# Graph network on one core: norms of the third and fourth layer from column statistics, degree scales moved ahead of the products

## What is computed

```python
def _layernorm(x):                       # over the 64 columns
    return (x - mean(x)) / sqrt(var(x) + 1e-5)

# block 1, in the kernel's edge phase: one 64x64 weight for each of 16 edge types
# block 2, three times (kernel layers 0, 1 and 2):
agg = segment_sum(h[src], dst) / max(cnt, 1)
h = agg @ Wl[i] + h @ Wr[i] + b[i]       # relu after the first two only
# block 3 (kernel layer 3):
feat_n = feat * rsqrt(out_deg)
h_src = feat_n[src]
copy_sum  = segment_sum(h_src, dst)
inner_sum = segment_sum(h_src * feat_n[dst], dst)
rst = (copy_sum @ weight1 + inner_sum @ weight2) * rsqrt(in_deg)
# block 4: two attention layers
```

## Time and profile before

| what | before |
|---|---|
| median of 3 runs | 6825.58 us (6820.51 to 6826.78) |
| the profiled execution, its time | 6816.61 us |
| the profiled execution, its span | 6814.9 us |
| busy: DVE, POOL, PE, ACT | 69%, 64%, 55%, 29% |
| third layer, first gather to first gather of the fourth | 2902.78 to 3559.78 us |
| fourth layer, first gather to the gather after it | 3559.78 to 4270.23 us |
| first layer, first to last gather | 1725.5 to 2254.1 us |
| third layer, first to last gather | 2902.8 to 3489.8 us |
| fourth layer, first to last gather | 3559.8 to 4190.3 us |

### The profile page before, as it was taken

One profiled execution on the slowest core, in us unless ns is written; L12 is line 12 of the kernel. 1 busy time (PEld: TensorE's weight loads), 2 busy tenths in 40 slices (PEclk: granted clock), 3 DMA queues, 4 the chain that ended last, 5 costly groups with the idle time before them and its releaser, 6 DMA issues. The chain is left out here.

```text
span 6814.9 us, 77215 instructions
## 1 busy us (share of the span) xinstructions
PE 3721.7 (55%) x19512; PEld 2540.9 (37%) x19512; DVE 4669.2 (69%) x16700; ACT 1956.3 (29%) x4823; POOL 4358.8 (64%) x4027
## 2 busy tenths in 40 slices
PE   3776888884588587723322333466378746661000
PEld 1443555552355455523322332355245423330000
DVE  7998999995455355446655676555699957776543
ACT  0000677775111111111111111122122258881000
POOL 5777777777677577577747784777200066664777
PEclk9999999997555556555555555777655678885555
DMA  1112344332233233234433433223133355552221
GB/s 37 49 48 75 125 157 145 111 104 82 71 105 89 66 105 89 82 108 129 129 111 92 122 107 109 87 88 94 68 139 129 137 114 130 131 138 75 83 88 71
DMA packets 413603, 684.89 MB, mean 100 GB/s; under 512 B 283685, under 2 KB 290444, under 8 KB 407978
## 3 DMA queue, kind: packets, MB, share of 16 engines
q1 hardware_dynamic: 282410, 542.14, 22.4%
q0 software_dynamic: 130944, 140.05, 10.4%
HBM read 310.94 MB, written 373.78 MB: 100 GB/s over the span
## 5 line engine op out<-in xcount | busy, mean ns | idle before, releaser
L697 POOL DMA_INDIRECT G<-states,srcq x1568 | 1761.7, 1124 | 528.0 <-issue 515.3
L1113 DVE TENSOR_TENSOR_SCAN R<-same,R,G 128x28 f32<-128x28 f32 x5376 | 990.0, 263 | 737.7 <-DMA G<-states,srcq 733.5
L1731 PE MATMUL PS<-ident,HH 128*128 128x128 f32 x2357 | 546.5, 392 | 1580.9 <-DVE HH L1275 684.9
L1731 PEld LDWEIGHTS PS<-ident,HH 128*128 128x128 f32 x2357 | 430.5, 215 | 1627.9 <-DVE HH L1275 700.5
L1998 ACT COPY AT<-PS 128x512 f32<-128x512 f32 (+1 forms) x494 | 287.7, 583 | 1983.5 <-PE PS L1731 1325.9
L697 POOL DMA_INDIRECT G<-states_xl,dsti x392 | 455.0, 1161 | 227.4 <-issue 122.0
L811 POOL DMA_INDIRECT out_nodes<-O,dstq x392 | 432.8, 1104 | 195.5 <-issue 123.3
L1746 PEld LDWEIGHTS PS<-WD,AT 128*128 128x128 f32 x2358 | 483.7, 305 | 123.6 <-issue 122.1
L1746 PE MATMUL PS<-WD,AT 128*128 128x64 f32 x2358 | 520.6, 398 | 1.1 <-ACT O L2009 0.7
L697 POOL DMA_INDIRECT G<-states,srci x392 | 421.7, 1076 | 124.3 <-issue 124.3
L697 POOL DMA_INDIRECT EE<-node_info,srcq x392 | 412.7, 1053 | 132.3 <-issue 132.3
(11 more groups left out here) (386 smaller groups left out, 9029.2 us busy)
## 6 DMA issues: line engine op xcount, KB each, us to landing
states<-O SPq DMA_DIRECT2D x70, 896.0 KB, 3.7
HH<-states SPq DMA_DIRECT2D x56, 896.0 KB
total<-R SPq DMA_DIRECT2D x56, 896.0 KB, 3.7
XB<-resid SPq DMA_DIRECT2D x42, 896.0 KB, 5.8
states<-HH SPq DMA_DIRECT2D x28, 896.0 KB
G<-states,srcq POOLq DMA_INDIRECT x1568
resid<-XB SPq DMA_DIRECT2D x28, 896.0 KB, 6.8
xl_of_src<-O SPq DMA_DIRECT2D x14, 1792.0 KB, 6.9
```

The costliest lines, as they stand in the source:

```text
L697: return pool.indirect_dma_start(to, None, table_, bass.IndirectOffsetOnAxis(ap=idx, axis=0), bounds_check=bound, oob_is_err=False).then_i ...
L1113: last = dve.tensor_tensor_scan(out=out_[:, order, f], data0=flags[:, order], data1=in_[:, order, f], initial=initial[:, f:f + 1], op0=ALU ...
L1731: last = pe.transpose(PS[:, 4 + k, q * P:(q + 1) * P], HH[:, b, (g * G4 + q) * D2:(g * G4 + q + 1) * D2], ident[:])
```

## The change

It touches the third and the fourth layer, the weights' loads and ACT's program.

- `new_states` takes the place of `new_state` for the 28-column chunks. DVE adds `O` to `XB`, takes mean and variance of each column by 28 `bn_stats` of 64 values, and works on tiles of 28 values after that. The norm itself is 28 `activation`s on ACT (`Relu(scale * x + bias)`, one for each column), spread in sevens over the group steps 4 to 7 of the next chunk's products (`normed_before`). The patch row keeps the old `norm`.
- The third layer's bias goes through PE, as in the first two: `lastb` and its addition are gone, `BS` has three rows.
- In the fourth layer ACT multiplies the loaded right halves by `rs_dst`, 28 `activation`s for each chunk, four to a group step of the chunk before (`scaled`). DVE waits for these (`s_rscaled`) and no longer for the load. `rs_in` is multiplied into the sums where the left halves are written, so that the copy and the scaling of `O` are gone.
- ACT's loops of these layers are written out, chunk by chunk.

```diff
@@ operands
                 if k < 3:
                     return tt(left, r, per_row(inv_in, i, INV_FT, n), ALU.mult)
-                step(tt(right, right, per_row(rs_dst, i, RSDST_FT, n), ALU.mult))
-                step(tt(right, right, r, ALU.mult))
-                return cast(left, r)
-
-            def new_state(k, layer, i, b, n):
-
-                o, xb = O[:, b, 0:n * D], XB[:, b, 0:n * D]
-                if k == 3:
-                    step(tt(cut(o), cut(o), per_row(rs_in, i, RSIN_FT, n), ALU.mult))
-                else:
-                    step(tt(cut(o), cut(o), lastb[:].unsqueeze(1).broadcast_to([P, n, D]), ALU.add))
+                step(tt(left, r, per_row(rs_in, i, RSIN_FT, n), ALU.mult))
+                if n == 1:
+                    step(tt(right, right, over(col(RSDST_FT), D), ALU.mult))
+                return tt(right, right, left, ALU.mult)
+
+            def new_states(k, layer, i, b):
+
+                total_, spread_, dev, inv, shift, diff = RLN
+                at = RNORMS + (k - 2) * CHUNKS + i
+                step(tt(XB[:, b, :], XB[:, b, :], O[:, b, 0:CD], ALU.add))
+                for j in range(C):
+                    last = dve.bn_stats(RSTATS[:, j, :], XB[:, b, j * D:(j + 1) * D])
+                step(last)
...
+                tt(spread_, spread_, diff, ALU.add).then_inc(s_vars, 1)
+                dve.wait_ge(s_devs, at + 1)
+                dve.wait_ge(s_done, before[layer, "done"] + i)
+                step(dve.reciprocal(inv, dev))
+                dve.scalar_tensor_tensor(out=shift, in0=total_, scalar=-0.5, in1=inv, op0=ALU.mult, op1=ALU.mult).then_inc(s_scales, 1)
@@ state
-                    dve.wait_ge(s_ld[b], before[layer, "ld"] + 16 * (it + 1))
+                    if k == 3:
+                        dve.wait_ge(s_rscaled, i + 1)
+                    else:
+                        dve.wait_ge(s_ld[b], before[layer, "ld"] + 16 * (it + 1))
@@ PE
-                how = (WD[:, k, :], BS[:, k, :], D) if k < 2 else (WD[:, k, :] if k == 2 else W12[:], None, D)
+                how = (WD[:, k, :], BS[:, k, :], D) if k < 3 else (W12[:], None, D)
@@ ACT
+                def scaled(i, groups):
+                    b = i % 2
+                    for g in groups:
+                        if g == 0:
+                            act.wait_ge(s_ld[b], before[layer, "ld"] + 16 * (i // 2 + 1))
+                        for j in range(g * G4, (g + 1) * G4):
+                            right = HH[:, b, j * D2 + D:(j + 1) * D2]
+                            last = act.activation(right, right, ACT.Copy, scale=rs_dst[:, i * C + j:i * C + j + 1])
+                        if g == GROUPS - 1:
+                            last.then_inc(s_rscaled, 1)
+
+                def normed_before(i, b, g):
...
+                    if g == 2:
+                        act.wait_ge(s_vars, at)
+                        act.activation(dev, spread_, ACT.Sqrt, bias=epsc[:], scale=1.0 / D).then_inc(s_devs, 1)
+                    if 4 <= g < 8:
+                        if g == 4:
+                            act.wait_ge(s_scales, at)
+                        for j in range((g - 4) * (C // 4), (g - 3) * (C // 4)):
+                            last = act.activation(O[:, b, j * D:(j + 1) * D], XB[:, b, j * D:(j + 1) * D], ACT.Relu,
+                                                  bias=shift[:, j:j + 1], scale=inv[:, j:j + 1])
+                        if g == 7:
+                            last.then_inc(s_done, 1)
```

More of the change, by code:

```diff
@@ L61 @@
 EPS = 1.0e-5
-WEIGHT_LOADS = 34
+WEIGHT_LOADS = 33
 HSLOT = 3 * (HI + 1) + 2 * 256
@@ L164, in build_program @@
         WG2 = sb("WG2", [P, D2])
[L165 removed]
+        BS = sb("BS", [1, 3, D])
         BG2 = sb("BG2", [1, D2])
@@ L306, in node_units @@
             return [(stage, w) for stage, w in made if 0 <= w < NGROUPS]
+        RSTATS = flat[2][:, 0:6 * C].rearrange("p (c k) -> p c k", k=6)
+        RLN = [flat[2][:, (6 + k) * C:(7 + k) * C] for k in range(6)]
+        RNORMS = len(NORMS)
         NROUNDS = NGROUPS + 4
@@ L332, in build_program @@
             plan(layer, ld=TURNS * 16, res=normed * TURNS * 16, st=(1 + normed) * TURNS * 16, tot=TURNS * 16, gath=TURNS * 16 * C,
-                 scan=CHUNKS, ready=CHUNKS + 1, group=GROUPS * CHUNKS + 1, done=(CHUNKS + 1) * normed, ln=normed * (CHUNKS + 1), carry=1,
+                 scan=CHUNKS, ready=CHUNKS + 1, group=GROUPS * CHUNKS + 1, done=(CHUNKS + 1) * normed, ln=normed, carry=1,
                  patch=(2 + normed) * 16, patched=(1 + normed) * 16)
@@ L1275, in operands, with new_first @@
                     return tt(left, r, per_row(inv_in, i, INV_FT, n), ALU.mult)
-                step(tt(right, right, per_row(rs_dst, i, RSDST_FT, n), ALU.mult))
-                step(tt(right, right, r, ALU.mult))
-                return cast(left, r)
-            def new_state(k, layer, i, b, n):
-                o, xb = O[:, b, 0:n * D], XB[:, b, 0:n * D]
-                if k == 3:
-                    step(tt(cut(o), cut(o), per_row(rs_in, i, RSIN_FT, n), ALU.mult))
-                else:
-                    step(tt(cut(o), cut(o), lastb[:].unsqueeze(1).broadcast_to([P, n, D]), ALU.add))
+                step(tt(left, r, per_row(rs_in, i, RSIN_FT, n), ALU.mult))
[9 more added lines that the diff above has]
+                step(last)
+                dve.wait_ge(s_scales, at)
+                tt(total_, RSTATS[:, :, 1], RSTATS[:, :, 4], ALU.add)
+                tt(spread_, RSTATS[:, :, 2], RSTATS[:, :, 5], ALU.add)
+                step(tt(diff, RSTATS[:, :, 1], RSTATS[:, :, 4], ALU.subtract))
+                step(dve.scalar_tensor_tensor(out=diff, in0=diff, scalar=D / 4.0, in1=diff, op0=ALU.mult, op1=ALU.mult))
+                tt(spread_, spread_, diff, ALU.add).then_inc(s_vars, 1)
[3 more added lines that the diff above has]
+                dve.scalar_tensor_tensor(out=shift, in0=total_, scalar=-0.5, in1=inv, op0=ALU.mult, op1=ALU.mult).then_inc(s_scales, 1)
+            def new_first(layer):
+                o, xb = O[:, 0, 0:D], XB[:, 0, 0:D]
                 step(tt(xb, xb, o, ALU.add))
-                norm(xb, o, n, before[layer, "ln"] + 1 + i).then_inc(s_done, 1)
+                norm(xb, o, 1, before[layer, "ln"] + 1).then_inc(s_done, 1)
             for b in range(2):
@@ L1313, in finish @@
                     dve.wait_ge(s_out, before[layer, "group"] + AHEAD + GROUPS * (i + 1))
-                    new_state(k, layer, i, b, C)
+                    new_states(k, layer, i, b)
                 def source_hots(i):
@@ L1365, in _ @@
                     dve.wait_ge(s_out, before[layer, "group"] + AHEAD + GROUPS * CHUNKS + 1)
-                    new_state(k, layer, CHUNKS, 0, 1)
+                    new_first(layer)
                 barrier()
@@ L2028, in free @@
                                                                 (i - b) // 2 * 16 * (1 + normed)))
-                def norm_before(i, g):
-                    if g == 2:
-                        square(C, before[layer, "ln"] + i)
-                    if g == 4:
-                        root(C, before[layer, "ln"] + i)
+                def scaled(i, groups):
[9 more added lines that the diff above has]
+                def normed_before(i, b, g):
+                    at = RNORMS + (k - 2) * CHUNKS + i
+                    total_, spread_, dev, inv, shift, diff = RLN
+                    if g == 2:
+                        act.wait_ge(s_vars, at)
[8 more added lines that the diff above has]
+                            last.then_inc(s_done, 1)
                 put = out_rows(ACT.Relu if k < 2 else ACT.Identity, free)
@@ L2039, in _, with beside @@
                     act.activation(rs_dst[:], SRC_P, ACT.Sqrt).then_inc(s_deg, 1)
-                if normed:
-                    products(layer, copy, put)(0, None, 0)
-                    body = products(layer, copy, put, norm_before)
-                    with act.Fori(0, TURNS - 1) as it:
-                        body(2 * it + 1, it, 1)
-                        body(2 * it + 2, it, 0)
-                    body(CHUNKS - 1, None, 1)
-                    norm(C, before[layer, "ln"] + CHUNKS)
+                if k == 3:
+                    scaled(0, range(GROUPS))
+                    for i in range(CHUNKS):
+                        def beside(i, g):
+                            if i + 1 < CHUNKS and g < GROUPS:
+                                scaled(i + 1, [g])
+                            if i:
+                                normed_before(i, (i - 1) % 2, g)
+                        products(layer, copy, put, beside)(i, i // 2, i % 2)
+                    for g in range(GROUPS + 2):
+                        normed_before(CHUNKS, 1, g)
+                elif k == 2:
+                    for i in range(CHUNKS):
+                        products(layer, copy, put, (lambda i, g: normed_before(i, (i - 1) % 2, g)) if i else None)(i, i // 2, i % 2)
+                    for g in range(GROUPS + 2):
```

(3 more changed lines are left out.)

13 lines of the change are left out of this document (6 added, 7 removed).

## The result

The changed kernel took 6704.73 us, the median of 4 runs (6699.06 to 6715.35), beside 6823.05 us of the kernel before (4 runs). The ratio is 0.9832 [0.9817, 0.9848]: 118 us less, where 115 were forecast. The profiled execution was the slowest of its four, 6715.35 us, so the two profiled spans differ by 101 us only. I first take those 101 us apart.

The account below looks back on a forecast made before the run. POOL's gathers were taken to bound the kernel, stretched by two-input DVE instructions and late every 112th. Terms -45 - 66 - 6 - 10 + 12.4 = -115 us from 6825.6 gave 6711 us; forecast 6695 to 6722, range 6692 to 6742.

Parts of the forecast that it names:

- third layer, stretching: Third layer's gathers: fewer two-input DVE instructions beside them, 5.3 us a chunk falling to 1.55, saves 45 us.
- fourth layer, stretching: Fourth layer's gathers: fewer two-input DVE instructions beside them, 8.4 us a chunk falling to 3.0, saves 66 us.
- late gathers, third: Third layer's every 112th gather: norm ends T + 27.4 (T: end of `operands`), store misses it by 5 us; saves 6.
- late gathers, fourth: Fourth layer's every 112th gather: norm ends T + 27 (T: end of `operands`), 7 us margin; saves 10 us.
- end of the third layer: Third layer's end: `finish` +10.3 us later from bias product and ACT's activations, then +2.4 to the store; +12.7.
- end of the fourth, patch: Fourth layer's end and patch rows: +2.8 us, less 2.6 for faster landing and 0.5 for the patch.
- The pair: Third layer: two two-input DVE instructions left back to back stretch a chunk's gathers by 1.55 us.
- The run of three: Fourth layer: three two-input DVE instructions back to back stretch a chunk's gathers by 2.2 us, from 2.06 to 2.5.
- rival (a): Third and fourth layer: stores still collide with late gathers, as when the norm comes earlier; about 6729 us, chance 0.18.
- Nothing else: Rest of the kernel: weight load, PE's bias products, ACT's body and new waits cost nothing, one wait 0.3 us.
- DVE's small instructions: Costed at nothing for POOL; rival: 0.1 to 0.2 us each, or the pair costs 2.2; 6735 us, chance 0.15.
- rival (c): Fourth layer: ACT, SP and the load of right halves become a ring, slower; 6855 us, chance 0.04.

Follow-up runs that it names:

- e10: Changed kernel with ScalarE's third and fourth layer as a loop over pairs of chunks, not written out; fast chip, 0.9836 of the kernel before.
- e4: Changed kernel with the last chunk's norm in third and fourth layer shared between ScalarE and VectorE; fast chip, 6708.08 us, 0.9831 of the kernel before.
- e2: Changed kernel plus one unused one-input DVE sum after each chunk's shift, third and fourth layer; slow chip, 1.0055 of the kernel before.
- e1: Changed kernel plus one unused two-input DVE minimum after each chunk's shift, third and fourth layer; slow chip, 1.0047 of the kernel before.
- e3: Changed kernel with two-input scalings of left halves and gathered rows written as 28 one-input column instructions; slow chip, 1.0167 of the kernel before.
- e7: Changed kernel without ScalarE's scaled copies of the fourth layer's right operands; slow chip, 8859.43 us, 0.9998 of the kernel before.
- e6: Kernel before with only the third layer's bias moved to a PE product; slow chip, 1.002 of the kernel before.
- b0_before: Kernel before, unedited, traced on a slow chip; gathers stretched 62 and 107 us in third and fourth layer, no whole time given under this label.
- c1_changed: Changed kernel, unedited, run again on another slow chip; 8895.80 us, 1.0031 of the kernel before.
- e9: Kernel before with ScalarE's third and fourth layer written out chunk by chunk instead of looped; fast chip, 0.9997 of the kernel before.

## Why the prediction was right, step by step

On the chip of the first measurement it held in size and, but for one late gather, by its own mechanism. Forecast and measured (the two profiled executions), in us:

| term | forecast | measured |
|---|---|---|
| third layer, stretching | -45 | 65.7 to 19.7: -46.0 |
| fourth layer, stretching | -66 | 105.5 to 50.1: -55.4 |
| late gathers, third | -6 | 12.3 to 10.7: -1.6 |
| late gathers, fourth | -10 | 15.9 to 5.7: -10.2 |
| end of the third layer | +12.7 | 70.0 to 79.5: +9.5 |
| end of the fourth, patch | -0.3 | 64.2 to 62.6: -1.6 |
| sum | -115 | -105.3 |

The end of the fourth is measured up to the patch's first gather. The two layers are 105.4 us shorter by their first gathers, so the table is complete. That 115 and the medians' 118 lie so close is luck in part: in the profiled pair the terms came to 10 us less than forecast. (The prediction gives two ranges, 6695 to 6722 us and 6692 to 6742; 6704.73 lies in both.) The medians have other executions in them: e10 and e4, profiled at 6700 and 6698 us, have 44.4 and 42.0 us of stretching in the fourth layer and 5.8 us of late gathers in each.

*Stretching.* The reason is shown: one-input work beside a gather costs it 0.00 us (e2), two-input work 1.25 (e1), and without it the first layer's stretching is gone (e3). The Trainium skill (page "SBUF — State Buffer", section "Who interferes with whom") infers that `tensor_tensor` leaves descriptor generation alone; e1's 2.85 us gather beside a `tensor_tensor` says otherwise for these indirect ones. The pair was sized rightly, 1.56 to 1.60 on average for 1.55. The run of three was sized too low, at 2.2: it took 2.74 (within 0.01) in all 12 chunks of each of the three traces (the changed kernel's, e10's, e4's). I had taken a value near the low end of 2.06 to 2.5, and it depends on where in the gather the run begins, 1.35 for the first gather here and 0.67 in the earlier trace rows. L1320 alone cost 0.6 to 0.7 in e4 and e10 and 1.2 in the changed kernel's trace, for 0.8. That is the 10 us by which the fourth layer fell short in this trace, and the 3 to 5 in the others.

*Late gathers, rival (a).* It came true for one of three in the third layer, and by the condition that it named. I had the norm's end at T + 27.4, and the stores come at T + 27.5 or 27.6 in eight of 13 chunks. In four, during whose products the clock was at its upper level for 3.4 us, they come at T + 24.5 to 24.7; in one, with 10.2 us of it, at T + 21.1, and that is the one ahead of the late gather. Rival (a) has "a higher PE clock gives T + 21". The trace shows that PE had stood idle for 10.49 us before that chunk's products, and for 10.52 before those of the chunk ahead of it, where the clock stayed low; why it rose is open. The margin was 5 us as forecast in most chunks, 1.1 to 2.2 in some, and the early store came 1.2 us before the chunk's last gather ended. e4's third layer has two such stores, at T + 21.1 and T + 21.2, and no late gather of the layer met them (2.0 us each), so it takes both an early store and a 112th gather. In the fourth layer a step failed: its stores come at T + 23.4 to 24.5 and not T + 27, a margin of 2.4 to 4.8 us for 7. Four scaled Copies take 1.07 us, not the 1.4 that I took from the earlier trace rows, which is 2.3 us over seven group steps; the rest I can't place. No store met a late gather there.

*Ends.* `finish` started at T + 25.3 in the third layer (forecast 28.2), 28.2 in e4. The granted clock was 0.74 from 3460 to 3467 and 0.50 after, so both its levels, 2.4 and 1.2 GHz, had a part of these products. That was named as a bound (T + 21 at the higher one). In e4 it was 0.50 throughout. 17.0 us to the store were forecast as 17.4.

*Nothing else.* This part held for the gathers: they took the same time without ACT's scalings (e7, 598.6 for 599.9 us), and the bias product brought no ring (e6). Both ran on a slow chip, so neither shows it for the fast one. DVE's small instructions and rival (c) showed no price in the traces of the fast chips.

*What it did not see* is that all this rests on DVE, ACT and PE having room. The earlier trace rows showed that room and I took it as given. On the slow chips there is none: the same 93 us of stretching less (169.3 to 75.8 us, b0_before and c1_changed) ended in a ratio of 1.003. Rival (c), a ring through ACT, is the nearest to what happened there, but its cause was not the one that I gave.

## What to carry to other kernels

Where GpSimd's gathers bound a stretch, give every whole-chunk VectorE instruction with two inputs a price of gather time (here 1.25 us alone, 1.6 for two in a row, 2.7 for three), and rewrite it as one-input work, as a product's bias or as scaled activations. Check first that the scans or whatever the gathers wait for have room for the longer form (in the first layer, on a slow chip, e3 saved 17 us of stretching and lost 18 in all). Time a kernel on more than one chip: a gain of 1.7% on one was a loss of some 0.3% on two others.

## What the runs showed of the hardware that I had not expected

- The same program took 6823 to 6827 us on two chips and 8865 to 8955 us on three, with instructions and gathers of the same length (1.00 us) but engines that stand without a releaser in the profile: DVE's scans 0.70 or 1.40 us apart instead of 0.18, DVE 439 instructions in the first 1000 us instead of 3183. The cause is open.
- A store that started 2.5 us before the idle time of a 112th gather made that idle time 6.65 us; with one that started 3.8 us after its beginning it was 1.92.
- Ten microseconds of the upper clock level moved a chunk's store from T + 27.5 to T + 21.1, and so into a late gather.
- A chunk's 64 scans took 26 us instead of 12 on the slow chips, in the layer whose VectorE program had grown from 84 to 114 instructions a chunk. That the one comes of the other isn't shown.
- Three two-input instructions in a row stretch the gathers by 2.04 to 3.19 us (e9), by where in a gather the run begins.
- 784 empty ScalarE instructions moved the time by nothing that can be told from 0 (1.0027 against 1.0031).
